# V of seven head pairs as three split passes over the tokens, turned by VectorE and laid down through DRAM

## The reference

```python
# x: (1, 2048, 128) f32; 16 heads of 64, D = 128
xn = layernorm(x)
q, k, v = xn @ Wq, xn @ Wk, xn @ Wv               # each (2048, 1024)
attn = softmax(q k^T * 64 ** -0.5)                # per head, 2048 x 2048
a = (attn @ v) @ Wo + bo
expert = argmax(softmax(xn @ router_w.T))         # 8 experts, one for each token
f = square(relu(xn @ expert_fc[expert])) @ expert_proj[expert].T
out = x + a + f
```

## Time and profile before

| what | value |
|---|---|
| median of 3 runs | 1335.16 us (1334.42 to 1336.8) |
| profiled execution, its own time | 1333.57 us |
| its span on the engines | 1331.8 us |
| PE busy | 1322.7 us (99%) |
| DVE busy | 1191.3 us (89%) |
| POOL busy | 1128.2 us (85%) |
| ACT busy | 708.3 us (53%) |
| DMA, q1 | 84736 packets, 79.38 MB |

### The profile page before, as it was taken

One profiled execution on the slowest core, in us unless ns is written; L12 is line 12 of the kernel. 1 busy time (PEld: TensorE's weight loads), 2 busy tenths in 40 slices (PEclk: granted clock), 3 DMA queues, 4 the chain that ended last, 5 costly groups with the idle time before them and its releaser, 6 DMA issues.

```text
span 1331.8 us, 20385 instructions
## 1 busy us (share of the span) xinstructions
PE 1322.7 (99%) x6338; PEld 867.1 (65%) x6338; DVE 1191.3 (89%) x1882; ACT 708.3 (53%) x1231; POOL 1128.2 (85%) x892
## 2 busy tenths in 40 slices
PE   8999999999999999999999999999999999999998
PEld 6765566766667766677666676666776666765554
DVE  7999999889888898898988989888998889989997
ACT  5654445654446644466544565444664445654453
POOL 7899999877888878798787988878988779888998
PEclk9999999999999999999999999999999999999999
DMA  5242212241123411233112432123311234011101
GB/s 143 55 106 71 67 44 56 63 102 48 43 58 78 100 35 42 59 93 85 42 43 50 102 77 52 34 58 93 93 35 35 66 78 100 11 37 42 35 17 40
DMA packets 85869, 82.78 MB, mean 62 GB/s; under 512 B 24513, under 2 KB 54913, under 8 KB 85761
## 3 DMA queue, kind: packets, MB, share of 16 engines
q1 hardware_dynamic: 84736, 79.38, 24.0%
q0 software_dynamic: 1024, 2.10, 0.6%
HBM read 27.00 MB, written 6.29 MB: 25 GB/s over the span
## 4 chain that ended last, share of the span: by engine, by line
PE 96%; DVE 2%; POOL 1%; issue 0%; DMA 0%; ACT 0%; DVEq 0%; ACTq 0%; POOLq 0%
PE OB L1231 33%; PE SB L1174 17%; PE MB L1202 17%; PE SB L1183 17%; PE XB L1259 2%; PE XB L1269 2%; PE XB L1155 2%; PE XB L1162 2%; DVE mx L827 1%; PE XB L1238 1%; PE XB L1239 1%; PE XB L1240 1%; POOL ex L592 0%; PE OB L1137 0%; DVE rd L992 0%
## 5 line engine op out<-in xcount | busy, mean ns | idle before, releaser
L558 POOL TENSOR_TENSOR acc<-acc,ex 128x512 f32<-128x512 f32 x690 | 911.5, 1348 | 29.1 <-ACT ex L698 1.1
L827 DVE TENSOR_REDUCE mx<-MB 128x1 f32<-128x512 f32 x992 | 639.4, 682 | 60.7 <-PE MB L1202 60.2
L698 ACT ACTIVATE ex<-SB 128x512 f32<-128x512 f32 x1024 | 607.8, 598 | 95.0 <-PE SB L1183 30.2
L1231 PE MATMUL OB<-ex,V 128*64 128x512 f32 x2048 | 447.2, 594 | 0.0
L1174 PE MATMUL SB<-Q,K 128*128 128x512 f32 x1024 | 410.0, 401 | 0.3 <-ACT ex L698 0.2
L1183 PE MATMUL SB<-Q,K 128*128 128x512 f32 x1024 | 399.3, 390 | 0.0
L1202 PE MATMUL MB<-K,Q 128*128 128x512 f32 x992 | 390.0, 394 | 1.0 <-DVE mx L827 0.7
L1231 PEld LDWEIGHTS OB<-ex,V 128*64 128x64 f32 x2048 | 144.0, 137 | 277.8 <-issue 274.2
L863 DVE TENSOR_TENSOR acc<-acc,ex 128x512 f32<-128x512 f32 x206 | 294.1, 1428 | 20.4 <-POOL acc L558 1.0
L726 ACT ACTIVATE osb<-OB 128x512 f32<-128x512 f32 x32 | 19.1, 597 | 449.1 <-PE OB L1231 449.1
L1174 PEld LDWEIGHTS SB<-Q,K 128*128 128x128 f32 x1024 | 192.5, 188 | 67.2 <-issue 27.6
(11 more groups left out here) (156 smaller groups left out, 637.2 us busy)
## 6 DMA issues: line engine op xcount, KB each, us to landing
Q<-high SPq DMA_DIRECT2D x124, 128.0 KB
K<-high SPq DMA_DIRECT2D x112, 128.0 KB, 2.3
Q<-low SPq DMA_DIRECT2D x62, 128.0 KB
rd<-rows_rd SPq DMA_DIRECT2D x62, 128.0 KB
K<-low SPq DMA_DIRECT2D x56, 128.0 KB, 2.4
w<-fc SPq DMA_DIRECT2D x23, 256.0 KB, 2.7
w<-projT SPq DMA_DIRECT2D x23, 256.0 KB, 3.0
sorted_x<-res SPq DMA_DIRECT2D x1, 1472.0 KB, 7.1
```

The lines of the kernel that those rows point to most:

```text
L558: pool.tensor_tensor(a[:, :], src[:, :], EX[h][kt][:, :], ALU.add).then_inc(done, 1)
L698: act.activation(EX[h][kt][:, :], SB[bank_of(n, 2 * kt + h)][:, :], ACT.Exp).then_inc(a_e[h], 1)
L827: dve.tensor_reduce(mx[:, m % 2, u:u + 1], MB[bank_of(m, i)][:, :], AX.X, ALU.max).then_inc(v_m, 1)
L1231: mm = pe.matmul(OB[own[h], :], V[:, k, own[h]], EX[h][k][:, :], start=(k == 0), stop=(k == NT - 1))
```

## The change

V of pairs 1 to 7 (28 chunks) is made like K: `split_product` with weights `whi_v` and `wlo_v`, three matmuls of 512 columns, one chunk per block (at kt = 8; block 1 has two, at kt = 8 and 10; no chunk in blocks 0 and 28 to 31), a pair ahead of its use. The result stands as heads x tokens, and has to be turned: DVE transposes `XB` in squares of 32 x 32 into a buffer in the dead `xT` (`turn_v`), SP stores the squares with four DMAs to `v_rows` in DRAM (`store_v`), so that the rows land as tokens, and at the start of the pair's first block one DMA loads all of V (`load_v`). ACT's copy into `V` goes; ACT's `split_w` and DVE's `low_w` get one more instruction each, of 128 columns, for `Wv`. The weights' second buffer moves into `xT`, so the load of pair 1's weights and their split come later in block 0. Pair 0's V is made as before.

```diff
-AT_V, AT_K, AT_LOW = (1, 2, 6, 8), (1, 6), 5
+AT_V, AT_K, AT_LOW = (8, 10), (1, 6), 5
+        whi_v, wlo_v = sb("whi_v", [P, P], F32R), sb("wlo_v", [P, P], F32R)
-        wraw = [sb(f"wraw{k}", [P, 3, P]) for k in range(2)]
+        wraw = [sb("wraw0", [P, 3, P]), xT[:, 0:3 * P].rearrange("p (k d) -> p k d", d=P)]
+        vT = [xT[:, k * QB:(k + 1) * QB] for k in (1, 2)]
...
             j, pair = n.off % JB, n // JB
-            if j == 0 and n.off and kt in AT_V:
-                return [("v", pair, AT_V.index(kt))]
-            if j in (1, 2) and n.off < NB - JB and kt in AT_K:
+            if n.off >= NB - JB:
+                return []
+            if n.off == 1 and kt in AT_V:
+                return [("v", pair + 1, AT_V.index(kt))]
+            if n.off and kt == AT_V[0]:
+                return [("v", pair + 1, j)]
+            if j in (1, 2) and kt in AT_K:
                 return [("k", pair + 1, 2 * (j - 1) + AT_K.index(kt))]
...
+                def store_v(pair, c):
+                    wait(sp, v_vT, pair.times(JB, c + 1 - JB))
+                    rows = v_rows[pair % 2][c * QB:(c + 1) * QB, :].rearrange("(b j) d -> j b d", j=SQ)
+                    for a in range(P // SQ):
+                        sp.dma_start(rows[:, :, a * SQ:(a + 1) * SQ],
+                                     vT[c % 2][a * SQ:(a + 1) * SQ, :].rearrange("j (b i) -> j b i", i=SQ)).then_inc(d_vT[c % 2], 16)
+                def load_v(pair):
+                    wait(sp, t_pv, pair.times(NT * JB))
+                    for k in range(2):
+                        wait(sp, d_vT[k], pair.times(2 * VD))
+                    sp.dma_start(V[:, :, :], v_rows[pair % 2].rearrange("(t p) d -> p t d", p=P)).then_inc(d_v, 16)
...
+                    if pair.off:
+                        wait(act, t_v, pair.times(JB))
+                        act.activation(whi_v[:, :], wraw[k][:, 2, :], ACT.Copy)
                     act.activation(whi[k][:, :, :], wraw[k][:, 0:2, :], ACT.Copy).then_inc(a_w, 1)
...
+                    if pair.off:
+                        dve.tensor_tensor(wlo_v[:, :], wraw[k][:, 2, :], whi_v[:, :], ALU.subtract)
                     dve.tensor_tensor(wlo[k][:, :, :], wraw[k][:, 0:2, :], whi[k][:, :, :], ALU.subtract).then_inc(v_w, 1)
+                def turn_v(pair, c):
+                    wait(dve, t_v, pair.times(JB, c + 1))
+                    wait(dve, d_vT[c % 2], (2 * (pair.off - 1) + c // 2) * VD)
+                    dve.transpose(vT[c % 2], XB[:, :]).then_inc(v_vT, 1)
...
+                    elif pair.off:
+                        take_spare(v_vT, pair.times(JB, c + 1 - JB))
+                        wait(pe, v_w, pair.times(1, 1))
+                        split_product(whi_v[:, :], wlo_v[:, :], c, XB).then_inc(t_v, 1)
```

More of the change, by code:

```diff
@@ L138, in layer @@
         xn_rows = nc.dram_tensor("xn_rows", (S, D), F32, kind="Internal").ap()
+        vT = [xT[:, k * QB:(k + 1) * QB] for k in (1, 2)]
+        v_rows = [nc.dram_tensor(f"v_rows{k}", (S, P), F32, kind="Internal").ap() for k in range(2)]
         q_start, q_low = EX[0][JB][:, :], EX[0][JB + 1][:, :].bitcast(F32R)
@@ L212, in layer @@
         d_k0 = [sem(f"d_k0{c}") for c in range(JB)]
+        v_vT, d_vT, d_v = sem("v_vT"), [sem(f"d_vT{k}") for k in range(2)], sem("d_v")
         d_q0, a_q0, g_q0, g_xn = sem("d_q0_"), sem("a_q0"), sem("g_q0"), sem("g_xn")
@@ L219, in layer @@
         TD = P // SQ * 16
-        QD, KD, MD = 6 * 16, 6 * 16, 2 * 16
+        QD, KD, MD, VD = 6 * 16, 6 * 16, 2 * 16, P // SQ * 16
         def units(n, kt, h):
@@ L355, in load_w @@
                     k, cols = pair % 2, bass.ds(address(sp, pair.place(P)), P)
-                    wait(sp, t_v, pair.times(JB, -JB))
+                    wait(sp, v_w, pair.times(1, -1))
+                    if pair.off == 1:
+                        wait(sp, t_v, JB)
                     for n, w in enumerate((wq, wk, wv)):
@@ L479, in first @@
                     store_xn(3)
-                    load_w(Lin(1))
                     spread_k0(1)
@@ L497, in one @@
                     pair = n // JB
+                    if n.off == 0:
+                        sp.wait_ge(t_lg, 1)
+                        load_w(pair + 1)
+                    if n.off and n % JB == 0:
+                        load_v(pair)
                     if n % JB == 1 and n.off < NB - 2 * JB:
@@ L518, in one @@
                             spread_k(*job[1:])
+                    for kt in AT_V:
+                        for job in kv_job(n, kt):
+                            store_v(*job[1:])
                     if n.off == 2:
@@ L717, in kv @@
                     else:
-                        wait(act, t_v, pair.times(JB, c + 1))
-                        wait(act, t_pv, pair.times(NT * JB))
+                        wait(act, t_v, c + 1)
                         act.activation(V[:, c * TB:(c + 1) * TB, :].rearrange("p t d -> p (t d)"),
@@ L805, in one @@
                         for job in kv_job(n, kt):
-                            kv(*job)
+                            if job[0] == "k":
+                                kv(*job)
                         if has_tile(n):
@@ L811, in one @@
                                 take_result(n - TILE0)
-                        if kt == 0 and n % JB == 0 and n.off < NB - JB:
+                        if kt == (0 if n.off else 6) and n % JB == 0 and n.off < NB - JB:
                             split_w(n // JB + 1)
@@ L1058, in one @@
                                 low_k(pair, c)
+                            else:
+                                turn_v(pair, c)
                         if kt == AT_LOW and n % JB == 0 and 0 < n.off < NB - JB:
@@ L1224, in times_v @@
                         wait(pe, a_o, n.times(1))
-                        wait(pe, a_v, (n // JB).times(JB, JB))
+                        if n.off < JB:
+                            wait(pe, a_v, JB)
+                        else:
+                            wait(pe, d_v, (n // JB).times(16))
                     for k in range(kt, kt + tiles):
@@ L1233, in times_v, with split_product @@
                     mm.then_inc(t_pv, tiles)
-                def split_product(w, par, c, XB):
+                def split_product(hi, lo, c, bank):
                     q = slice(c * QB, (c + 1) * QB)
-                    pe.matmul(XB[:, :], whi[par][:, w, :], xhi[:, q], start=True, stop=False)
-                    pe.matmul(XB[:, :], wlo[par][:, w, :], xhi[:, q], start=False, stop=False)
-                    return pe.matmul(XB[:, :], whi[par][:, w, :], xlo[:, q], start=False, stop=True)
+                    pe.matmul(bank[:, :], hi, xhi[:, q], start=True, stop=False)
+                    pe.matmul(bank[:, :], lo, xhi[:, q], start=False, stop=False)
+                    return pe.matmul(bank[:, :], hi, xlo[:, q], start=False, stop=True)
                 def make_q(m, bank=XB):
@@ L1245, in make_q @@
                     wait(pe, v_w, (m // JB).times(1, 1))
-                    split_product(0, (m // JB) % 2, m % JB, bank).then_inc(t_q, 1)
+                    split_product(whi[m // JB % 2][:, 0, :], wlo[m // JB % 2][:, 0, :], m % JB, bank).then_inc(t_q, 1)
                 def make_kv(kind, pair, c, bank=XB):
@@ L1252, in make_kv @@
                         wait(pe, v_w, pair.times(1, 1))
-                        split_product(1, pair % 2, c, bank).then_inc(t_k, 1)
-                    else:
-                        take_spare(a_v, pair.times(JB, c + 1))
-                        wait(pe, d_w[pair % 2], (pair // 2).times(48, 48))
+                        split_product(whi[pair % 2][:, 1, :], wlo[pair % 2][:, 1, :], c, bank).then_inc(t_k, 1)
+                    elif pair.off:
+                        take_spare(v_vT, pair.times(JB, c + 1 - JB))
+                        wait(pe, v_w, pair.times(1, 1))
+                        split_product(whi_v[:, :], wlo_v[:, :], c, XB).then_inc(t_v, 1)
+                    else:
+                        take_spare(a_v, c + 1)
+                        wait(pe, d_w[0], 48)
                         for k in range(TB):
```

## The result

The changed kernel takes 1339.07 us (median of 10 executions, 1338.86 to 1340.24) against 1335.28 us for the kernel before, measured beside it (10 executions, 1334.06 to 1336.8). The ratio is 1.0031 with a 95% interval of 1.0023 to 1.0039: slower, by 3 to 5 us. The forecast was 1340.1. The profiled execution took 1339.35 us, with a span of 1337.6, which is 5.8 above the one of before; of these, 1.7 are there because the profiled execution of before was quicker than its median, and 0.3 because that of the changed kernel was slower than its own.

A forecast was written before the change was run, and what follows sets the result against it. PE, busy 99% of the span, was taken as the bound, with DVE next at 89%. The terms -5.9 + 6.5 + 3.2 + 1.1 = +4.9 us on 1335.16 gave 1340.1 us, range 1331.5 to 1342.5.

The forecast's parts named there:

- The step that carries the sum: Blocks 4, 8, 12, 16, 20, 24: DVE's second back-to-back subtraction waits for another whole POOL add; 6.5 us in five, 3.2 in block 4.
- blocks 0 and 1: End of block 0: the extra subtraction puts DVE's adds one turn back, 1.6 us, so block 1 starts late; cost 1.1 us.
- PE's saving, 5.9 us: 28 chunks of V: a split product takes 0.68 us instead of 0.89, saving 0.21 each, 5.9 us in all.
- low_w in five blocks, 1.3 each: Blocks 8, 12, 16, 20, 24: the second subtraction loses its turn to POOL, unit 15 waits 1.3 us; 6.5 us in all.
- The rival that DVE keeps its turn: Both subtractions run in one gap between POOL's adds; sum -3.3 us, 1331.9 us; chance 0.19.
- Block 4, 3.2 us: Block 4 loses its covering chunks: 1.1 us stand with the late fold, plus 2.1 for the two subtractions without slack.
- The transposes, 0: DVE's transposes of XB take 0.71 us each, covered by the product before them, which leaves DVE 0.68 without maxima; cost 0.
- DMA and SP, 0: Stores take 4 us of the queues per chunk, V's load is allowed 8; both land before they are needed; cost 0.
- Block 28 "I take 0": Block 28 loses its chunks and has no low_w: cost up to 0.3 us, taken as 0.

The follow-up runs named there:

- experiment 1: Changed kernel with its two low_w subtractions (128 and 256 wide) made one of 384 columns, and ACT's two roundings one: 1331.62 us, ratio 0.9975 to the kernel before.
- experiment 2: Changed kernel without V's low-part subtraction after pair 1, later pairs using pair 1's low part: 1332.17 us, ratio 0.9979.
- experiment 3: Changed kernel with the 128-wide subtraction of pairs 2 to 7 reading one operand from an idle PSUM bank: 1332.04 us, ratio 0.9981 to the kernel before.
- experiment 5: Kernel before the change, with its chunks of V at kt = 1, 2, 8, 11 instead of 1, 2, 6, 8: 1337.47 us, ratio 1.0022.
- experiment 7: On top of experiment 1, block 0's low_w stands at kt = 10 instead of ahead of the six adds at the block's end: 1332.15 us.
- experiment 8: On top of experiment 7, one add of POOL given to DVE in block 28 and one in block 29: 1329.79 us, ratio 0.997 to the kernel before.
- experiment 4: Changed kernel with DVE's transposes on 32 of the 512 columns, the rest of V not written: 1339.99 us, ratio 1.0037.
- experiment 6: Changed kernel with POOL's 16 indirect fetches of expert results replaced by one plain DMA from SP: 1338.34 us, ratio 1.003 to the kernel before.

## Why the prediction was right, point by point

The step that carries the sum, a second turn at POOL's adds in six blocks, is shown. One term (blocks 0 and 1) came out by another way than the one told, and one loss (blocks 29 and 30) was not in the sum at all. So part of the agreement of 4.9 with the measured 3.8 is luck.

- **PE's saving, 5.9 us.** Right. A product costs 0.65 to 0.71 in the blocks j = 1 to 3, and block 28, which only lost its chunks, took the 37.5 us that were worked out.
- **low_w in five blocks, 1.3 each.** Right in mechanism and size. The ends of the two subtractions, 0.16 and 0.28 behind POOL's adds, are the 0.15 and 0.29 of the working, the second takes 1.51, and the blocks take 41.3 us as forecast. Experiments 1, 2 and 3 take the second turn away in three ways and each gives back 1.25 to 1.33 a block. The rival that DVE keeps its turn (first in the prediction's list, though it is once called the second) does not happen in any of these blocks.
- **Block 4, 3.2 us.** 41.2 where 41.4 was forecast. Experiment 1 splits it: the second turn is 1.2, and the rest stays, with 40.0 against the 38.2 that PE would need. The prediction puts this rest down to the late fold and one subtraction together; no run parts the two.
- **Blocks 0 and 1, 1.1 us.** The size is right, the way there is not, and that is luck. Block 1 became 2.4 us longer; 1.4 of it are its two products, 1.0 is the wait. DVE's adds at the end of block 0 did begin 1.65 us later (67.75 against 66.10), but not because the second subtraction lost its turn: that one took 0.41. The first one missed a gap and took 2.34 (last section). One subtraction alone does the same. In experiment 5, whose block 0 is that of the kernel before, the only subtraction took

```profile
65.30 2.19 DVE L873 TENSOR_TENSOR wlo<-wraw,whi 128x256 fp32r<-128x256 f32 x1
```

  where it took 1.00 before, and block 1 was 0.5 us longer for it. At this place the first subtraction missed a gap in seven of the eight profiled executions that have it there (1.83 to 2.37 us); the kernel before is the eighth, in the one execution that was profiled. Experiments 7 and 8, which have no subtraction there, have no such wait in block 1 (41.2, which is 39.9 and two products). So the 1.0 us is the price of the subtractions at the end of block 0. But experiment 4, with two of them there, lost 0.6 in block 1 (41.8), hardly more than experiment 5 with one (0.5). How much of the 1.0 the change brought is open.
- **The transposes, 0.** Right: 706 ns against the 0.71 taken, and experiment 4 moves no block behind block 1.
- **DMA and SP, 0.** Right, and the prices were put too high. The stores land in 1.9 us in the median, and V's load in 6.1 to 6.8 where 8 were allowed. These are the page's row of the stores, and the answer on the load's line:

```profile
v_rows<-xT SPq DMA_DIRECT2D x112, 64.0 KB, 1.9
```

```profile
DMA to landing us min/median/max: 6.1/6.2/6.8
```

  q1 went from 84736 packets to 147568, and nothing waited for one of them. The Trainium skill, "DMA: Bandwidth & Descriptors", section "Specifications", says that transfers under 512 bytes don't reach line rate and are read, changed and written back. Whether that happened in these stores no run here shows; 64 KB in pieces of 128 bytes landed in 1.9 us.
- **Block 28 "I take 0": the loss that the sum lacks.** It held for block 28 itself and for nothing behind it. That PE gets faster was reckoned a gain in full, and I did not ask what next was late. POOL was, with 2.0 us of air, and PE ran 3.6 us ahead: blocks 29 and 30 took 1.2 us more. Only experiment 6 (POOL freed) and experiment 8 (POOL's work moved) give them back.

The sum over blocks 1 to 30 of the two profiled executions is +5.5 us where 4.9 was forecast: the 1.2 of blocks 29 and 30, less some 0.6 spread over the terms above. The last block is 0.3 longer as well. The medians are 3.8 apart, the two profiled executions 5.8. So the forecast stands 1.1 above what the medians show and 0.9 below what the profiles show.

What stays open is how much of the medians' difference is due to the start phase and to the gap missed at the end of block 0 (both below), and why one subtraction alone takes 0.7 to 0.9 us in one kernel and 1.36 in another: only that it hangs on POOL's phase is shown, not what sets the phase.

## What to carry to other kernels

Where two engines keep each other waiting, as DVE's subtractions and POOL's adds do here, count instructions and not elements: one subtraction of 384 columns cost 0.94 us where one of 128 and one of 256 cost 2.2, and merging them turned a loss of 0.3% into a gain of 0.25%. With one operand in PSUM the subtraction did not wait at all (0.28 us inside POOL's add). When work is taken from the engine that bounds a kernel, look at the stretch behind it for the engine with the least air: the 3.6 us taken from one block came back as 1.2 us in the next two, and one add handed over in each of two blocks mended that.

## What the runs showed of the hardware that was not expected

The turns are not strictly alternate. At the end of block 0 of the changed kernel:

```profile
64.83 1.29 POOL L592 TENSOR_TENSOR acc<-acc,ex 128x512 f32<-128x512 f32 x1
65.15 2.34 DVE L911 TENSOR_TENSOR wlo_v<-xT,whi_v 128x128 fp32r<-128x128 f32 x1
66.05 1.29 POOL L592 TENSOR_TENSOR acc<-acc,ex 128x512 f32<-128x512 f32 x1
67.41 0.41 DVE L912 TENSOR_TENSOR wlo<-xT,whi 128x256 fp32r<-128x256 f32 x1
67.48 1.47 POOL L592 TENSOR_TENSOR acc<-acc,ex 128x512 f32<-128x512 f32 x1
```

The first subtraction was there in time for the gap between two adds (66.12) and did not get it: it took 2.34 us, until POOL's next add was over at 67.34. Then the second ran at once in the same gap, in 0.41, and this time POOL waited (1.47). So one waiter may lose a turn that it came in time for, and two instructions may pass in one gap. The same pair at kt = 5 never did this: there the first took the next gap in all six blocks, and the second waited. What parts the two places no run here shows.

The granted clock in the start phase differs between executions. The windows from 20 to 40 and 40 to 80 us of experiment 1:

```profile
20.00:40.00 20.00, 19.84 (x110) 14.35 (x109) 17.54 (x24) 8.40 (x14) 18.36 (x16) 0.91 0.46 110
40.00:80.00 40.00, 39.77 (x172) 24.08 (x171) 35.95 (x58) 18.98 (x35) 32.98 (x26) 0.96 0.31 82
```

and the first of them in the changed kernel:

```profile
20.00:40.00 20.00, 19.84 (x124) 14.58 (x123) 18.13 (x25) 8.63 (x15) 18.35 (x16) 1.00 0.46 110
```

PE is busy 19.84 us in both, but at 0.91 of 2.4 GHz in the mean it gets through 110 matmuls and not 124, so a part of the stretch ran at 1.2 GHz. Block 1 began 2.9 us later there (79.86 against 76.97). It is not the edit: experiment 4, whose block 0 is that of the changed kernel, shows the same.

```profile
20.00:40.00 20.00, 19.85 (x110) 14.46 (x108) 17.37 (x24) 8.47 (x14) 18.35 (x16) 0.91 0.46 110
```

Its block 1 began at 79.92. That is as much as several of the effects in this study, and the reason why they were read from block lengths behind block 1.
